# Last phase of a GNN + FFN kernel: VectorE's instruction for x2's mean is taken out, and two pieces of its step stand later

## Chip, core, metric

The kernel runs on one core of a Trainium2 chip. The metric is the device time of one execution in microseconds (us); it is given as the median of a few runs, and one further execution was taken with the hardware profiler.

## What is computed

10,000 nodes of 512 features pass a layer norm, three rounds of a graph network (a sum over each node's edges, two 512x512 products, ReLU, a norm over the row), and a residual sum. Then comes a feed-forward layer with 8 experts, of which each node takes its best two, a second residual sum, and a last layer norm inside it. Cut to what the change touches:

```python
def layer_norm(x, g, b):
    m = x.mean(-1, keepdims=True)
    v = ((x - m) ** 2).mean(-1, keepdims=True)
    return (x - m) / jnp.sqrt(v + EPS) * g + b
...
x = x + gnn(layer_norm0(x), src, dst, ...)       # this sum is x2 in the kernel
xn = layer_norm0(x)                              # mean and variance of x2
x = x + ffn(xn, Wg, W1, b1, W2, b2, ...)
```

## The kernel before

The edges are sorted by target node and cut into 79 tiles of 127 edges; all work goes tile by tile, 128 rows by 512 columns. Phases 0, 1 and 2 are the layer norm and the first graph rounds with their products. This case is about the last phase, number 3, from about 1490 us to the end: it sums the last round's rows, forms x2, and does the whole feed-forward layer.

Each engine has its own program, an unrolled loop over steps. In step k an engine calls a fixed list of small functions, each for the tile k plus an offset: the list `[(-9, hs), ..., (3, x2), ...]` at the end of VectorE's block is its order of a step, written out by hand. Engines meet only through semaphores (`wait_ge`, `then_inc`), and each runs its own instructions strictly in order. Tiles go in groups of four: some functions do a whole group at once, in the step in which its last tile comes by, so four steps in a row differ, and the pattern repeats every four.

What a step does, with the lines as the profile has them and the names of the tiles (buffers are reused, so a row of the trace may call x2's tile `area`, and the small scalars `w_n`):

- **POOL (GpSimd)**: `gather` (L814, rows of the neighbours by an indirect DMA), `by_node` (L830, rows of x; waits for an earlier tile's x2, whose buffer it refills), `norm3` (L881, and L883, which writes `scl`), once a group `pow_of_group` (L873, waits for `group_vars`), `zr_of` (L890, L893, which writes `zr`), `put_out` (L902, the result's rows, an indirect DMA that adds).
- **VectorE (DVE)**: `hs` (L1636), once a group `confidences` (L1618 to L1626, which writes W128), `carry_lo` (L1461), `combine` (L1473, writes R), `x2` (L1522: x2 = RR * scl + X, both in SBUF, with the row's sum as a second result, read out by a short instruction of its own), `x2_mean` (L1530), `logits` (L1573), `flo` (L1643, reads two SBUF tiles), once a group `group_scales` (L1558 to L1562), `largest` (L1580), `one_hot` (L1452), `largest_index` (L1586), once a group `gaps` and `group_vars` (L1542, L1544), then `z_stats` (L1648), `hots`, `z_mean_var` (L1654), `result` (L1671), `z_gain` (L1661), `xlo` (L1568).
- **ScalarE (ACT)**: `relu` (L994), `sum_squares3` (L1030), `weights_in` (L1072), `x2_deviations` (L1038: the squares of x2 less its mean, and their sum), `xn` (L1047), `xhi` (L1056), `gelu` (L1080), `carry_hi` (L983), `fhi` (L1087).
- **TensorE (PE)**: `aggregate` (L1827, L1828), `down` (L553 into psS, L1893, L1894), `turn_w` (L1856, which waits for W128), `up` (L1869, L1871), `gate` (L553 into psA), `spread_w` (L1879).

A loop between POOL and VectorE runs through this: `x2` waits for `scl` of its tile from POOL's L883, and POOL's L830, some instructions later, waits for an older x2. `down` waits for `flo`; `largest` waits for `logits`.

Of the kernel before, what the change touches and what calls it, by code (L numbers as in the profile page):

```python
# [5 lines left out]
ALU = mybir.AluOpType  # L6
ACT = mybir.ActivationFunctionType
# [10 lines left out]
D = 512  # L18
# [5 lines left out]
T = -(-E // EPT)  # L24
# [28 lines left out]
LN_EPS = 1e-5  # L53
# [69 lines left out]
def run_plan(tiles, stages, jobs, windows=(), run=0):  # L123
    offs = [o for o, _ in stages]
    begin, end = -max(max(offs), 0), max([tiles - min(min(offs), 0)] + [j[0] + 1 for j in jobs])
    cuts = sorted({begin, end} | {j[0] for j in jobs} | {e for w in windows for e in w[:2]})
    for a, b in zip(cuts, cuts[1:]):
        for at, f, arg in jobs:
            if at == a:
                f() if arg is None else f(arg)  # L130
        run_steps(tiles, stages + [(0, f) for x, y, f in windows if x <= a and b <= y], a, b, run)
# [28 lines left out]
def after(eng, sem, n):  # L160
    if n > 0:
        eng.wait_ge(sem, n)
# [57 lines left out]
class FfnSems:  # L220


    def __init__(self, sem):
        self.out = [sem(f"f3_out{i}") for i in range(2)]
        self.x2 = sem("f3_x2")
        self.mean = sem("f3_mean")
        self.dev = sem("f3_dev")
        self.ssf = sem("f3_ssf")
        self.lnv = sem("f3_lnv")
        self.pw = sem("f3_pw")  # L230
        self.nb = sem("f3_nb")
        self.xn = sem("f3_xn")
        self.xhi = sem("f3_xhi")
        self.xlo = sem("f3_xlo")
        self.ht = [sem(f"f3_ht{i}") for i in range(HT_RING)]
        self.gate = sem("f3_gate")
        self.logit = sem("f3_logit")
        self.top = sem("f3_top")
        self.topi = sem("f3_topi")
        self.gap = sem("f3_gap")  # L240
        self.hot = sem("f3_hot")
        self.th = sem("f3_th")
        self.w48 = sem("f3_w48")
        self.pad = sem("f3_pad")
        self.wt = sem("f3_wt")
        self.wtt = sem("f3_wtt")
        self.up = sem("f3_up")
        self.gel = sem("f3_gel")
        self.spread = sem("f3_spread")
        self.hs = sem("f3_hs")  # L250
        self.fhi = sem("f3_fhi")
        self.flo = sem("f3_flo")
        self.down = sem("f3_down")
        self.bnz = sem("f3_bnz")
        self.aggz = sem("f3_aggz")
        self.zv = sem("f3_zv")
        self.zr = sem("f3_zr")
        self.o1 = sem("f3_o1")
        self.prior = [sem(f"f3_prior{i}") for i in range(2)]
        self.o = sem("f3_o")  # L260


def build(nc, x, src, dst, W_self, W_neigh, b, Wg, W1, b1, W2, b2, ln_g, ln_b, out_g, out_b, out):
    with ExitStack() as ctx:
# [247 lines left out]
        def lt(n, dt=F32, parts=P):  # L512

            at = late_at[0]
            late_at[0] = at + n
            v = late[0:parts, at:at + n]
            return v if dt is F32 else v.bitcast(dt)

        sumx = lt(2 * GROUP).rearrange("p (i t) -> p i t", i=2)
        nmean = lt(2 * GROUP).rearrange("p (i t) -> p i t", i=2)  # L520
        ssx = lt(2 * GROUP).rearrange("p (i t) -> p i t", i=2)
        vvb = lt(4 * GROUP).rearrange("p (i t two) -> p i t two", i=2, two=2)
        pwb = lt(4 * GROUP).rearrange("p (i t two) -> p i t two", i=2, two=2)
# [389 lines left out]
        def _(act):  # L913
# [118 lines left out]
            def x2_deviations(t):  # L1032

                t = t.own
                i, j = t.group % 2, t.place
                act.wait_ge(f3.mean, (t + 1).n)
                after(act, f3.lnv, t.group - 1)
                act.activation(bmat.rearrange("p c n -> p (c n)"), X2[t.slot(X2_RING)], ACT.Square, bias=nmean[:, i, j:j + 1],  # L1038
                               accum_out=ssx[:, i, j:j + 1]).then_inc(f3.dev, 1)

            def xn(t):

# [51 lines left out]
        def _(dve):  # L1094
# [352 lines left out]
            def one_hot(t, l):  # L1447

                s = ph[l]
                i = t.slot(GRING)  # L1450
                after(dve, s.agg, (t + (1 - GRING)).n)
                dve.tensor_scalar(Sm[i][:, :], iota16[:, :], colT[:, t.t:t.t + 1], rowval[:, 0:1],  # L1452
                                  ALU.is_equal, ALU.mult).then_inc(s.smat, 1)

            def carry_lo(t, l):
                s = ph[l]
                i, o = t.slot(2), (t + 1).slot(GRING)
                if t.t == T - 1:
                    return
                dve.wait_ge(s.chi, (t + 1).n - t.run)  # L1460
                dve.scalar_tensor_tensor(G[o][0:1, D:2 * D], (psA3 if l == 3 else psA)[i][0:1, :], 1.0 / CARRY,  # L1461
                                         G[o][0:1, 0:D], ALU.mult, ALU.subtract).then_inc(s.clo, 1)

            def combine(t, l):
                s = ph[l]
                i = t.slot(2)
                if l == 1:
                    dve.wait_ge(s.x[i], t.landed(2))
                else:
                    dve.wait_ge(s.xs[i], Tile(t.t, l - 2).landed(2))  # L1470
                dve.wait_ge(s.agg, (t + 1).n)
                after(dve, s.rr, (t + -1).n)
                dve.scalar_tensor_tensor(R[i][:, :], (psA3 if l == 3 else psA)[i][:, :], invs[:, l - 1, t.t:t.t + 1],  # L1473
                                         Sl[i][:, :], ALU.mult, ALU.add).then_inc(s.r, 1)
# [40 lines left out]
            def x2(t):  # L1515
                i, q = t.slot(2), t.slot(X2_RING)
                dve.wait_ge(s.sc, (t + 1).n)
                dve.wait_ge(s.rr, (t + 1).n)
                t = t.own
                dve.wait_ge(s.xg[i], t.landed(2))  # L1520
                after(dve, f3.o, (t + (1 - X2_RING)).n)
                dve.scalar_tensor_tensor(X2[q], RR[i][:, :], scl[:, i:i + 1], X[i][:, :], ALU.mult, ALU.add,  # L1522
                                         accum_out=sumx[:, t.group % 2, t.place:t.place + 1]).then_inc(f3.x2, 1)

            def x2_mean(t):
                t = t.own
                i, j = t.group % 2, t.place
                dve.wait_ge(f3.x2, (t + 1).n)
                after(dve, f3.dev, GROUP * (t.group - 1))
                dve.tensor_scalar(nmean[:, i, j:j + 1], sumx[:, i, j:j + 1], -1.0 / D, None, ALU.mult  # L1530
                                  ).then_inc(f3.mean, 1)

            def group_vars(t):

                t = t.own
                if not t.ends_group:
                    return
                g, k = t.group, t.place + 1
                i = g % 2
                dve.wait_ge(f3.dev, (t + 1).n)  # L1540
                after(dve, f3.pw, g - 1)
                dve.tensor_scalar(vvb[:, i, 0:k, 0], ssx[:, i, 0:k], (1.0 + LN_EPS) / (D * LN_UP ** 2),  # L1542
                                  (LN_EPS / LN_UP) ** 2, ALU.mult, ALU.add)
                dve.tensor_scalar(vvb[:, i, 0:k, 1], ssx[:, i, 0:k], 1.0 / D, LN_EPS, ALU.mult, ALU.add  # L1544
                                  ).then_inc(f3.lnv, 1)

            def group_scales(t):

                t = t.own
                if not t.ends_group:  # L1550
                    return
                g, k = t.group, t.place + 1
                i, q = g % 2, g % 4
                dve.wait_ge(f3.pw, g + 1)

                after(dve, f3.xn, GROUP * (g - 1))
                after(dve, f3.zv, GROUP * (g - 3))
                link(dve.scalar_tensor_tensor(r2b[:, q, 0:k], pwb[:, i, 0:k, 1], 0.5 * CONF_UP / LN_UP, pwb[:, i, 0:k, 0],  # L1558
                                              ALU.mult, ALU.mult))
                dve.scalar_tensor_tensor(ezb[:, q, 0:k], r2b[:, q, 0:k], downs[:, FINAL:FINAL + 1], r2b[:, q, 0:k],  # L1560
                                         ALU.mult, ALU.mult)
                dve.tensor_tensor(nbb[:, i, 0:k], nmean[:, i, 0:k], pwb[:, i, 0:k, 0], ALU.mult).then_inc(f3.nb, 1)  # L1562

            def xlo(t):
                t = t.own
# [108 lines left out]
            def sev_last(k):  # L1674
                sev(late_tile(k, 2), 2)

            run_plan(T, [(-9, hs), (-5, confidences), (4, lambda t: carry_lo(t, 3)), (4, lambda t: combine(t, 3)), (3,
                          x2), (3, x2_mean), (-4, logits), (-9, flo), (2, group_scales), (-4, largest), (6, lambda t:
                          one_hot(t, 3)), (-4, largest_index), (-4, gaps), (3, group_vars), (-10, z_stats), (-4, hots),
                          (-10, z_mean_var), (-11, result), (-10, z_gain), (-1, xlo)],  # L1680
                     [(max(k - LATE_AHEAD, -1) - 3, sev_last, k) for k in range(LATE[2])], run=2)


# [247 lines left out]
```

## Time and profile before

| | us |
|---|---|
| median of 3 runs (lowest, highest) | 2128.86 (2127.16, 2131.32) |
| profiled execution, its own time | 2129.58 |
| span of that execution in the trace | 2127.5 |
| busy in the span: PE, DVE, ACT, POOL | 1992.0, 1671.8, 1015.8, 1269.9 |

The profiled execution's time is 2.08 us above its span, and 0.72 us above the median. Busy shares are means over phases with different limits; what matters below is read from the last phase alone.

### The profile page before, as it was taken

To read this page: it belongs to the slowest core of one execution; us is meant where nothing else is said; L and a number is where in the kernel's file an instruction comes from. 1 tells how busy PE (TensorE), PEld (TensorE's weight loads), DVE (VectorE), ACT (ScalarE), POOL (GpSimd) and SP (SyncE) were. 2 spreads that over 40 slices of the span, in tenths; PEclk is the share of its full clock that TensorE was granted. 3 is DMA by queue.
4 is the path that set the end of the run, shared out by engine and by line. 5 is a ranking of instruction groups with operands and counts; after the bars stand their busy time and mean duration, and the time that the engine had idled before them with its cause. 6 is when DMAs were issued, how large, how long until landed. Compare 5 with 4: busy or idle time off the path is not lost.

```text
span 2127.5 us, 42838 instructions
## 1 busy us (share of the span) xinstructions
PE 1992.0 (94%) x14663; PEld 1101.4 (52%) x14669; DVE 1671.8 (79%) x4112; ACT 1015.8 (48%) x1794; POOL 1269.9 (60%) x1396
## 2 busy tenths in 40 slices
PE   6999899997999999997999999988699999999996
PEld 3454444443444444443444444443477777777774
DVE  7778986655777787775888877775699999999985
ACT  4444333332444443343444434444777777677751
POOL 2884116784666666563444444443678888888865
PEclk9999999998999999999999999999899999999998
DMA  6664338974788777874788888874779998999963
GB/s 206 169 169 130 121 139 138 142 127 120 200 197 202 193 205 192 195 196 144 236 246 252 250 241 233 240 222 157 206 161 176 176 179 177 177 175 184 172 103 49
DMA packets 321183, 382.67 MB, mean 180 GB/s; under 512 B 190554, under 2 KB 190728, under 8 KB 320968
## 3 DMA queue, kind: packets, MB, share of 16 engines
q1 hardware_dynamic: 260151, 214.50, 43.3%
q0 software_dynamic: 60816, 165.43, 31.5%
q8 instruction: 119, 1.95, 0.4%
q14 instruction: 97, 0.79, 0.1%
HBM read 175.81 MB, written 165.31 MB: 160 GB/s over the span
## 4 chain that ended last, share of the span: by engine, by line
PE 45%; POOL 22%; issue 11%; DMA 9%; DVE 8%; ACT 4%; SPq 1%; POOLq 0%; DVEq 0%; ACTq 0%
PE psS L553 19%; PE psY L553 19%; DMA w_n<-HH 7%; POOL out_dram L902 4%; POOL node_info L737 4%; POOL X L830 3%; PE psT L1770 2%; POOL zr L893 2%; PE psY L1869 2%; POOL G L814 2%; POOL area L814 2%; DVE R L1473 2%; POOL scl L883 1%; POOL w_n L873 1%; PE psA L1828 1%
## 5 line engine op out<-in xcount | busy, mean ns | idle before, releaser
L553 PE MATMUL psY<-w_n,HT 128*128 128x512 f16 x1812 | 423.0, 384 | 11.8 <-ACT HT L967 9.1
L553 PE MATMUL psS<-w_s,HT 128*128 128x512 f16 x1812 | 415.8, 379 | 1.4 <-DVE SB L1364 1.4
L553 PEld LDWEIGHTS psY<-w_n,HT 128*128 128x128 f16 x1812 | 177.7, 99 | 231.9 <-ACT HT L967 12.8
L994 ACT ACTIVATE RR<-R 128x512 f32<-128x512 f32 x237 | 149.5, 631 | 304.9 <-DVE R L1473 304.8
L846 POOL DMA_INDIRECT y_rows<-YB,poutT x158 | 161.4, 1021 | 193.2 <-DVE YB L1352 161.0
L553 PEld LDWEIGHTS psS<-w_s,HT 128*128 128x128 f16 x1812 | 173.8, 98 | 197.3 <-DVE SB L1364 1.9
L1364 DVE SCALAR_TENSOR_TENSOR SB<-psS,downs,bias 128x512 f32<-128x512 f32 x237 | 177.7, 750 | 79.2 <-PE psS L553 77.2
L839 POOL TENSOR_TENSOR scl<-ssm,halfpow 128x1 f32<-128x1 f32 x158 | 88.6, 561 | 223.0 <-DVE ssm L1491 223.0
L553 PE MATMUL psS<-w_w,raw 128*128 128x512 f16 x948 | 217.6, 379 | 0.8 <-ACT raw L1087 0.8
L553 PE MATMUL psY<-w_n 128*128 128x512 f16 x852 | 195.8, 380 | 13.6 <-DMA w_n<-HH 13.3
L1352 DVE SCALAR_TENSOR_TENSOR YB<-psY,YB 128x512 f16<-128x512 f32 x237 | 162.5, 685 | 54.3 <-ACT YB L960 53.5
L553 PE MATMUL psS<-w_s,w_n 128*128 128x512 f16 x852 | 195.5, 379 | 0.0
L1005 ACT ACTIVATE HH<-RR,scl 128x512 f16<-128x512 f32 x158 | 114.1, 722 | 150.1 <-POOL scl L839 150.1
L960 ACT ACTIVATE YB<-psY 128x512 f16<-128x512 f32 x237 | 138.2, 583 | 70.9 <-PE psY L553 60.6
L1497 DVE SCALAR_TENSOR_TENSOR HH<-RR,scl,HH 128x512 f16<-128x512 f32 x158 | 118.7, 751 | 57.4 <-ACT HH L1005 57.4
L951 ACT ACTIVATE HH<-R 128x512 f16<-128x512 f32 x79 | 49.7, 629 | 225.3 <-DVE R L1328 225.3
L902 POOL DMA_INDIRECT out_dram<-raw,poutT x79 | 147.3, 1864 | 15.3 <-issue 14.5
L814 POOL DMA_INDIRECT G<-y_rows,srcT x120 | 126.9, 1058 | 48.9 <-issue 31.2
L553 PEld LDWEIGHTS psS<-w_w,raw 128*128 128x128 f16 x948 | 92.0, 98 | 109.8 <-ACT raw L1087 1.1
L758 POOL TENSOR_TENSOR scl<-ssm,halfpow 128x1 f32<-128x1 f32 x79 | 61.6, 781 | 145.3 <-DVE ssm L1321 140.1
L1473 DVE SCALAR_TENSOR_TENSOR R<-psA,invs,Sl 128x512 f32<-128x512 f32 x198 | 144.4, 729 | 0.7 <-DMA Sl<-self_rows,pinT 0.7
L553 PEld LDWEIGHTS psY<-w_n 128*128 128x128 f16 x852 | 81.0, 98 | 120.7 <-DMA w_n<-HH 27.0
(327 smaller groups left out, 4094.6 us busy)
## 6 DMA issues: line engine op xcount, KB each, us to landing
self_rows<-SB SPq DMA_DIRECT2D x236, 256.0 KB, 2.0
Sl<-self_rows SPq DMA_DIRECT2D x158, 256.0 KB
area<-in_x_dram SPq DMA_DIRECT2D x78, 256.0 KB, 4.7
y_rows<-YB SPq DMA_DIRECT2D x78, 256.0 KB, 4.5
out_dram<-obb SPq DMA_DIRECT2D x78, 256.0 KB, 4.3
raw<-in_L_gnn_W_neigh_dram SPq DMA_DIRECT2D x12, 256.0 KB, 3.8
raw<-in_L_gnn_W_self_dram SPq DMA_DIRECT2D x12, 256.0 KB
y_rows<-YB,poutT POOLq DMA_INDIRECT x158
```

The costliest lines, as they stand in the source:

```text
L553: mm = eng.matmul(acc, lhs[:, a, c, :], w[:, bpart, c, :], start=(c == 0 and n == 0), stop=(stop and c == KC - 1 and n == 2))
L814: pool.indirect_dma_start(G[i][:, :], None, Yd[l - 1][:, :], bass.IndirectOffsetOnAxis(ap=srcT[:, t.t:t.t + 1], axis=0), bounds_check=node ...
L839: pool.tensor_tensor(scl[:, i:i + 1], ssm[:, i:i + 1], halfpow[:, 1:2], ALU.pow).then_inc(s.sc, 1)
L846: pool.indirect_dma_start(Yd[l][:, :], bass.IndirectOffsetOnAxis(ap=poutT[:, t.t:t.t + 1], axis=0), YB[i][:, :], None, bounds_check=node_l ...
L902: pool.indirect_dma_start(out[:, :], bass.IndirectOffsetOnAxis(ap=poutT[:, t.t:t.t + 1], axis=0), OUT[i], None, bounds_check=node_limit, o ...
L960: act.activation(YB[i][:, 0:D], psY[i][:, :], ACT.Copy, scale=k).then_inc(s.yhi, 1)
L994: act.activation(RR[i][:, :], R[i][:, :], ACT.Relu).then_inc(s.rr, 1)
L1005: act.activation(HH[i][:, 0, :], RR[i][:, :], ACT.Copy, scale=scl[:, i:i + 1]).then_inc(s.hhi, 1)
L1352: dve.scalar_tensor_tensor(YB[i][:, D:2 * D], psY[i][:, :], k, YB[i][:, 0:D], ALU.mult, ALU.subtract).then_inc(s.ylo, 1)
L1364: dve.scalar_tensor_tensor(SB[i][:, :], psS[i][:, :], downs[:, c:c + 1], bias[:, l, :], ALU.mult, ALU.add).then_inc(s.sev, 1)
L1473: dve.scalar_tensor_tensor(R[i][:, :], (psA3 if l == 3 else psA)[i][:, :], invs[:, l - 1, t.t:t.t + 1], Sl[i][:, :], ALU.mult, ALU.add).th ...
L1497: dve.scalar_tensor_tensor(HH[i][:, 1, :], RR[i][:, :], scl[:, i:i + 1], HH[i][:, 0, :], ALU.mult, ALU.subtract).then_inc(s.hlo, 1)
```

## The change

The mean of x2 is no longer formed. ScalarE squares the sum less 512 times the value, which is the deviation times 512 with its sign turned; `group_vars` divides by 512 cubed in place of 512, and `group_scales` multiplies the sum by -1/512 where it took the mean. ScalarE now waits for x2's semaphore. In VectorE's list, `x2` moves from behind `combine` to behind `flo`, and `group_vars` from ahead of `z_stats` to behind `z_gain`.

```diff
-                act.wait_ge(f3.mean, (t + 1).n)
+                act.wait_ge(f3.x2, (t + 1).n)
                 after(act, f3.lnv, t.group - 1)
-                act.activation(bmat.rearrange("p c n -> p (c n)"), X2[t.slot(X2_RING)], ACT.Square, bias=nmean[:, i, j:j + 1],
-                               accum_out=ssx[:, i, j:j + 1]).then_inc(f3.dev, 1)
+                act.activation(bmat.rearrange("p c n -> p (c n)"), X2[t.slot(X2_RING)], ACT.Square, bias=sumx[:, i, j:j + 1],
+                               scale=-float(D), accum_out=ssx[:, i, j:j + 1]).then_inc(f3.dev, 1)
...
                 after(dve, f3.o, (t + (1 - X2_RING)).n)
+                after(dve, f3.dev, GROUP * (t.group - 1))
                 dve.scalar_tensor_tensor(X2[q], RR[i][:, :], scl[:, i:i + 1], X[i][:, :], ALU.mult, ALU.add,
                                          accum_out=sumx[:, t.group % 2, t.place:t.place + 1]).then_inc(f3.x2, 1)
-
-            def x2_mean(t):
-                t = t.own
-                i, j = t.group % 2, t.place
-                dve.wait_ge(f3.x2, (t + 1).n)
-                after(dve, f3.dev, GROUP * (t.group - 1))
-                dve.tensor_scalar(nmean[:, i, j:j + 1], sumx[:, i, j:j + 1], -1.0 / D, None, ALU.mult
-                                  ).then_inc(f3.mean, 1)
...
-                dve.tensor_scalar(vvb[:, i, 0:k, 0], ssx[:, i, 0:k], (1.0 + LN_EPS) / (D * LN_UP ** 2),
+                dve.tensor_scalar(vvb[:, i, 0:k, 0], ssx[:, i, 0:k], (1.0 + LN_EPS) / (D ** 3 * LN_UP ** 2),
...
-                dve.tensor_tensor(nbb[:, i, 0:k], nmean[:, i, 0:k], pwb[:, i, 0:k, 0], ALU.mult).then_inc(f3.nb, 1)
+                dve.scalar_tensor_tensor(nbb[:, i, 0:k], sumx[:, i, 0:k], -1.0 / D, pwb[:, i, 0:k, 0],
+                                         ALU.mult, ALU.mult).then_inc(f3.nb, 1)
...
-            run_plan(T, [(-9, hs), (-5, confidences), (4, lambda t: carry_lo(t, 3)), (4, lambda t: combine(t, 3)), (3,
-                          x2), (3, x2_mean), (-4, logits), (-9, flo), (2, group_scales), (-4, largest), (6, lambda t:
-                          one_hot(t, 3)), (-4, largest_index), (-4, gaps), (3, group_vars), (-10, z_stats), (-4, hots),
-                          (-10, z_mean_var), (-11, result), (-10, z_gain), (-1, xlo)],
+            run_plan(T, [(-9, hs), (-5, confidences), (4, lambda t: carry_lo(t, 3)), (4, lambda t: combine(t, 3)), (-4, logits), (-9, flo), (3, x2), (2, group_scales), (-4, largest), (6, lambda t:
+                          one_hot(t, 3)), (-4, largest_index), (-4, gaps), (-10, z_stats), (-4, hots),
+                          (-10, z_mean_var), (-11, result), (-10, z_gain), (3, group_vars), (-1, xlo)],
```

The first place is on VectorE, in the step in which a group's variances are formed, in the middle of the last phase. Before (L1522 is `x2`, L1530 the mean, L1573 `logits`, L1643 `flo`, L1542 and L1544 `group_vars`, L1671 `result`):

```order
L1522 SCALAR_TENSOR_TENSOR area,w_n<-RR,scl,X 128x512
L1530 TENSOR_SCALAR w_n<-w_n 128x1
L1573 SCALAR_TENSOR_TENSOR w_n<-psA,downs,bgb 128x8
L1643 TENSOR_TENSOR raw<-raw 128x512
L1580 MAX w_n<-w_n 128x8
L1452 TENSOR_SCALAR Sm<-iota,colT,rowval 128x128
L1586 MAX_INDEX w_n<-w_n 128x8
L1542 TENSOR_SCALAR w_n<-w_n 128x4
L1544 TENSOR_SCALAR w_n<-w_n 128x4
L1648 BN_STATS st6b<-psS 128x6
L1654 BN_AGGR zm<-st6b 128x2
L1671 SCALAR_TENSOR_TENSOR raw<-area,zr 128x512
```

The same place now. Line numbers have shifted: `logits` is L1565, `flo` L1635, `x2` L1521, `result` L1663, `z_gain` L1653, `group_vars` L1533 and L1535:

```order
L1565 SCALAR_TENSOR_TENSOR w_n<-psA,downs,bgb 128x8
L1635 TENSOR_TENSOR raw<-raw 128x512
L1521 SCALAR_TENSOR_TENSOR area,w_n<-RR,scl,X 128x512
L1572 MAX w_n<-w_n 128x8
L1450 TENSOR_SCALAR Sm<-iota,colT,rowval 128x128
L1578 MAX_INDEX w_n<-w_n 128x8
L1640 BN_STATS st6b<-psS 128x6
L1646 BN_AGGR zm<-st6b 128x2
L1663 SCALAR_TENSOR_TENSOR raw<-area,zr 128x512
L1653 SCALAR_TENSOR_TENSOR area<-psS,zm,ogb 128x512
L1533 TENSOR_SCALAR w_n<-w_n 128x4
L1535 TENSOR_SCALAR w_n<-w_n 128x4
```

`logits` and `flo` now come ahead of `x2`, one instruction is gone, and the variances have moved behind four more instructions.

The second place is on VectorE one step later, where the group's scales are formed (L1558 to L1562). Before, from `combine` on:

```order
L1473 SCALAR_TENSOR_TENSOR R<-psA,invs,Sl 128x512
L1522 SCALAR_TENSOR_TENSOR area,w_n<-RR,scl,X 128x512
L1530 TENSOR_SCALAR w_n<-w_n 128x1
L1573 SCALAR_TENSOR_TENSOR w_n<-psA,downs,bgb 128x8
L1643 TENSOR_TENSOR raw<-raw 128x512
L1558 SCALAR_TENSOR_TENSOR w_n<-w_n 128x4
```

And now (`combine` is L1471, the scales begin at L1549):

```order
L1471 SCALAR_TENSOR_TENSOR R<-psA,invs,Sl 128x512
L1565 SCALAR_TENSOR_TENSOR w_n<-psA,downs,bgb 128x8
L1635 TENSOR_TENSOR raw<-raw 128x512
L1521 SCALAR_TENSOR_TENSOR area,w_n<-RR,scl,X 128x512
L1549 SCALAR_TENSOR_TENSOR w_n<-w_n 128x4
```

The scales stood behind `flo` and now stand right behind `x2`; `x2` has `flo` right ahead of it. The programs of ScalarE, POOL, TensorE and SyncE keep their order.

## Rows read from the trace of the kernel before

**Rows 1.** Busy us (instructions) of each engine, granted clock, DMA, 1600 to 2000 us.

```profile
core 0: us, PE busy (x) PEld busy (x) DVE busy (x) ACT busy (x) POOL busy (x), PEclk, DMA share, GB/s
1600.00:2000.00 400.00, 387.53 (x4959) 289.89 (x4957) 382.00 (x1102) 282.46 (x605) 346.64 (x389) 1.00 0.95 178
```

**Rows 2.** TensorE's waits from 1600 us on: total us, times, longest.

```profile
PE psT L1856 <- DVE w_n L1626: 13.4, 14, 1.2
```

**Rows 3.** VectorE's waits, 1600 to 2010 us.

```profile
DVE area L1522 <- POOL scl L883: 6.9, 14, 0.5
DVE w_n L1542 <- ACT bmat L1038: 4.1, 14, 0.3
```

**Rows 4.** POOL's waits, 1600 to 2010 us (one of four lines, all of this kind).

```profile
POOL out_dram L902 <- issue: 10.2, 55, 0.2
...
```

**Rows 5.** Timeline of POOL, `pow_of_group`, first and last full group: start, us.

```profile
1607.25 1.64 POOL L873 TENSOR_TENSOR w_n<-w_n,powers 128x8 f32<-128x8 f32 x1
...
1995.03 1.64 POOL L873 TENSOR_TENSOR w_n<-w_n,powers 128x8 f32<-128x8 f32 x1
```

**Rows 6.** Timeline of TensorE, the starts of two successive `down`.

```profile
1857.00 2.75 PE L553 MATMUL psS<-w_w,raw 128*128 128x512 f16 x12
...
1864.17 2.75 PE L553 MATMUL psS<-w_w,raw 128*128 128x512 f16 x12
```

**Rows 7.** Timeline of POOL within one group.

```profile
1854.11 0.58 POOL L883 TENSOR_TENSOR scl<-ssm,halfpow 128x1 f32<-128x1 f32 x1
...
1855.09 0.84 POOL L893 TENSOR_TENSOR zr<-zv,halfpow 128x1 f32<-128x1 f32 x1
1856.11 1.87 POOL L902 DMA_INDIRECT out_dram<-raw,poutT  x1 [0.18 <-issue]
...
1861.05 0.57 POOL L883 TENSOR_TENSOR scl<-ssm,halfpow 128x1 f32<-128x1 f32 x1
...
1869.04 0.57 POOL L893 TENSOR_TENSOR zr<-zv,halfpow 128x1 f32<-128x1 f32 x1
1869.79 2.17 POOL L902 DMA_INDIRECT out_dram<-raw,poutT  x1 [0.18 <-issue]
```

**Rows 8.** Timeline of VectorE in the same group.

```profile
1854.72 0.77 DVE L1522 SCALAR_TENSOR_TENSOR area<-RR,scl,X 128x512 f32<-128x512 f32 x1 [0.49 <-POOL scl L883]
1855.43 0.08 DVE L1522 DVE_READ_ACCUMULATOR area<-RR,scl,X 128x1 f32 x1
1855.54 0.15 DVE L1530 TENSOR_SCALAR w_n<-w_n 128x1 f32<-128x1 f32 x1
1855.61 0.21 DVE L1573 SCALAR_TENSOR_TENSOR w_n<-psA,downs,bgb 128x8 f32<-128x8 f32 x1
1855.74 0.68 DVE L1643 TENSOR_TENSOR raw<-raw 128x512 f16<-128x512 f32 x1
1856.34 0.16 DVE L1580 MAX8 w_n<-w_n 128x8 f32<-128x8 f32 x1
...
1860.79 0.73 DVE L1473 SCALAR_TENSOR_TENSOR R<-psT,invs,Sl 128x512 f32<-128x512 f32 x1
1861.65 0.78 DVE L1522 SCALAR_TENSOR_TENSOR area<-RR,scl,X 128x512 f32<-128x512 f32 x1
...
1869.01 0.73 DVE L1473 SCALAR_TENSOR_TENSOR R<-psA,invs,Sl 128x512 f32<-128x512 f32 x1
1869.66 0.73 DVE L1522 SCALAR_TENSOR_TENSOR area<-RR,scl,X 128x512 f32<-128x512 f32 x1
...
1876.88 0.73 DVE L1522 SCALAR_TENSOR_TENSOR area<-RR,scl,X 128x512 f32<-128x512 f32 x1
```

**Rows 9.** Timelines of VectorE and POOL elsewhere: L883 under a VectorE instruction, L902 alone.

```profile
1567.15 0.73 DVE L1671 SCALAR_TENSOR_TENSOR raw<-area,zr 128x512 f32<-128x512 f32 x1
...
1567.30 1.02 POOL L883 TENSOR_TENSOR scl<-ssm,halfpow 128x1 f32<-128x1 f32 x1
...
2095.10 1.62 POOL L902 DMA_INDIRECT out_dram<-raw,poutT  x1 [0.19 <-issue]
```

More of the change, by code:

```diff
@@ L225, in __init__ @@
         self.x2 = sem("f3_x2")
-        self.mean = sem("f3_mean")
         self.dev = sem("f3_dev")
@@ L519, in build @@
         sumx = lt(2 * GROUP).rearrange("p (i t) -> p i t", i=2)
-        nmean = lt(2 * GROUP).rearrange("p (i t) -> p i t", i=2)
         ssx = lt(2 * GROUP).rearrange("p (i t) -> p i t", i=2)
@@ L1541, in group_vars @@
                 after(dve, f3.pw, g - 1)
-                dve.tensor_scalar(vvb[:, i, 0:k, 0], ssx[:, i, 0:k], (1.0 + LN_EPS) / (D * LN_UP ** 2),
+                dve.tensor_scalar(vvb[:, i, 0:k, 0], ssx[:, i, 0:k], (1.0 + LN_EPS) / (D ** 3 * LN_UP ** 2),
                                   (LN_EPS / LN_UP) ** 2, ALU.mult, ALU.add)
-                dve.tensor_scalar(vvb[:, i, 0:k, 1], ssx[:, i, 0:k], 1.0 / D, LN_EPS, ALU.mult, ALU.add
+                dve.tensor_scalar(vvb[:, i, 0:k, 1], ssx[:, i, 0:k], 1.0 / D ** 3, LN_EPS, ALU.mult, ALU.add
                                   ).then_inc(f3.lnv, 1)
```

## The prediction

> **What bounds the kernel now.** I read the busy shares of the last phase first. From 1600 to 2000 us TensorE is busy for 387.5 of 400 us and VectorE for 382 [rows 1], both at the full 2.4 GHz grant. That names two candidates and decides nothing, so I went to the waits of each engine. TensorE stalls 14 times, 13.4 us in all, each time at `turn_w` for W128 from VectorE [rows 2]: once a group. VectorE waits 6.9 us in 14 places for `scl` from POOL, and 4.1 us in 14 for ScalarE's sum of squares in `group_vars` [rows 3]. POOL waits for nobody: all four lines of its waits read "issue", gaps that follow each of its DMA instructions [rows 4]. So although POOL has the lowest busy figure of the three, it sets the pace: POOL delays `x2`, VectorE then delays W128, TensorE stalls. The pace is 13 groups between the first and the last `pow_of_group`, (1995.03 - 1607.25) / 13 = 29.83 us a group [rows 5]. TensorE alone would need 4 x 7.17 = 28.68 [rows 6]. The difference, 1.15 us a group, is all that any change outside TensorE can return here: 14 x 1.15, some 16 us.
>
> **Why POOL's instructions differ in length.** The same `zr` instruction takes 0.57 us at 1869.04 and 0.84 at 1855.09 [rows 7]. In the second case `x2`, which reads two SBUF tiles, is running until 1855.49 [rows 8], and `zr` ends 0.44 later. `put_out` takes 1.62 alone [rows 9], 1.87 at 1856.11 with `flo` running until 1856.42, and 2.17 at 1869.79 with `x2` until 1870.39 [rows 7, 8]: both end 1.56 to 1.57 after the VectorE instruction. `scl` took 1.02 instead of 0.57 when `result`, running to 1567.88, covered its start: it ended 0.44 after it [rows 9]. So a POOL instruction that starts under a VectorE instruction with two SBUF inputs is held until that one ends. This coupling decides the case, because the change moves `x2` against `flo`, and POOL's pace follows. By the Trainium skill (SBUF — State Buffer, Who interferes with whom), a VectorE instruction with two SBUF inputs contends with GpSimd instructions that read SBUF, and the page infers that descriptor generation, which needs the write side, is not stalled by a tensor_tensor. The first half agrees with `zr`'s 0.84 against 0.57; the second does not agree with `put_out`'s 1.87 against 1.62 under a tensor_tensor. By the page taken alone, moving `flo` away from `put_out` would return nothing there; by the rows it returns 0.25 in each of two steps of a group.
>
> **The change part by part.** (a) The mean: from the read-out of `x2`'s sum to `logits` is 0.18 us, of which the mean's own start-to-start is 0.07 [rows 8]. The read-out stays, so the saving lies between 0.07 and 0.18; I take 0.12, four times a group. (b) `logits` and `flo` ahead of `x2`: 0.13 and 0.60 by their starts [rows 8]. In the step at 1854.72 VectorE stands 0.49 us for `scl`; it can now do these two in that time. (c) `group_vars` behind `z_gain`: its wait of 4.1 / 14 = 0.29 goes. Its result then comes at most 3.7 us after `x2` (`x2` to `largest` 0.77, `largest` to `combine` 1856.34 to 1860.79, less three instructions of over 0.5 that stay behind it). (d) ScalarE's square has the same size, and `group_scales` the same count; I cost them at nothing. `flo` and `logits` come earlier, so TensorE, which waits for them, gains cover. Later is `x2`, for `by_node` on POOL and the squares on ScalarE. POOL runs more than a step behind here (it waits for no semaphore [rows 4]). Before POOL is saturated it does wait for `x2`, once, so its whole chain may start up to 0.73 later; against that, from `scl` to W128 VectorE now has `logits`, `flo` and the mean less, 0.85. I net these to nothing.
>
> **VectorE's new pace.** `x2` to `x2` over the four steps is 6.93, 8.01, 7.22 and, by the repeat after 29.81, 7.65 [rows 8]. Out of these come waits: 0.21 in the first (`combine` to `x2` is 0.86 there, 0.65 at 1869.01), 0.35 in the third (c, with the gap beside it), 0.55 in the fourth (0.49 and the same gap), and the mean's 0.12 in each: 6.60, 7.89, 6.75, 6.98, sum 28.22. This is below TensorE's 28.68.
>
> **POOL against it.** Put 0 at the end of the `scl` instruction at 1854.69, and count on.
> - Second step. `x2` starts at 0.03 and holds `zr`, which ends at 1.24 as before; `put_out` starts at 1.42, no longer under `flo`, and takes 1.62. From its end to the next `scl` instruction is 1861.05 - 1857.98 = 3.07 [rows 7], so that starts at 6.11. `flo` now stands 0.60 ahead of `x2`: it starts at 0.03 + 6.60 - 0.60 = 6.03, and runs to 6.71. The `scl` instruction starts under it, and ends at 6.71 + 0.44 = 7.15. `x2` starts at 7.18 where it could have at 6.63: a new wait of 0.55, made by the move itself.
> - Third step. `x2` comes at 7.18 + 7.89 = 15.07, `flo` at 14.47; the `scl` instruction starts at 7.15 + 6.11 = 13.26 and is clear. `put_out` starts 1.14 after its end (0.39 + 0.57 + 0.18), under `flo`, and ends at 16.7, or at 17.4 if it has to let `x2` pass too.
> - Fourth step. The `scl` instruction starts 3.07 later, at 19.8 or 20.5; `flo` comes at 21.2: clear. `pow_of_group` (1.64 [rows 5]) follows at 20.4 or 21.0; the variances are there by 15.07 + 3.7 = 18.8. `x2` at 21.82.
> - First step of the next group. `x2` holds POOL until 22.56, `put_out` starts near 23.55, the `scl` instruction 1.62 + 3.07 later at 28.24. `flo` starts at 21.82 + 6.98 - 0.60 = 28.20. These are 0.04 apart, less than I know them. If it is held, `x2` comes at 29.35; if not, at 28.80.
>
> So a group costs 28.22 plus 0.55 for each step in which `flo` covers the start of the `scl` instruction, and no less than 28.68. No such step: 28.68, a gain of 1.15 a group. One: 28.77, gain 1.06. Two: 29.32, gain 0.51. Three: 29.87, no gain. Four: 30.42, a loss of 0.59. The working gives one for certain and a second on a knife's edge, so I take it in half of the groups: 0.78 a group, times 13, is 10.2 us. From the profiled execution (2129.58) that makes 2119.4; against the median, which is 0.72 lower, 2118.7. I say 2119.
>
> **Rivals.** *TensorE takes over.* If POOL's and VectorE's phases settle so that `flo` misses the `scl` instruction, both lie below 28.68, and the stall at `turn_w` is gone: 13 to 14 groups x 1.15, 2113 to 2114. For it: only 0.08 separates the two starts in the second step. Against: the delay is self-repairing, since after a hit both move on by the same amount, and meet again. *Nothing comes of it.* POOL's chain is full, what the change removes is on VectorE, and `put_out`'s saving is paid back by `flo` in front of `scl`: three hits a group, 2129 to 2130. For it: every wait removed is on an engine that does not set the pace. *Slower.* `flo` and `x2` side by side hold POOL for 1.3 us in a row where two shorter stretches stood apart; if `flo` meets `scl` in all four steps, 13 x 0.59 = 8 us more, 2137. It decides from the fourth hit on; against it stands the third step, where `confidences` pushes `flo` 1.2 us past. A price without a row here is that of POOL slipping in between `flo` and `x2`: nothing, or the 0.66 of `put_out` above, which the next hit swallows.
>
> **How the numbers follow.** About 0.2% (4.3 us) is what a measurement of this kernel can tell from no change. TensorE's pace 0.28; one or two hits a group, the forecast, 0.40; nothing 0.19; slower 0.13. Faster is the first two, 0.68; same 0.19; slower 0.13. The forecast's own range is 2114.5 to 2122.5 (one hit to two in each group). The range to be held reaches from TensorE's floor to just past no gain, 2113 to 2131.
>
> **What would show it.** Right: the pitch of `pow_of_group` falls from 29.83 to 28.8 to 29.3; TensorE's stalls at `turn_w` shrink from 0.96 to between 0.1 and 0.6; `put_out` behind the first step's `x2` is 1.6; some `scl` instructions read about 1.1 instead of 0.57, each with `flo` over its start; the wait of L1542 for ScalarE is gone. If no `scl` is long and TensorE stands for nobody, the first rival holds. If POOL still shows no wait and 29.8, the second. The prediction is wrong at its root if POOL's instructions keep their lengths whatever VectorE runs beside them.

## The result, and the profile after

The changed kernel is slower: 2156.99 us (median; 2155.21 to 2161.5) against 2128.44 (the three runs ahead of the prediction and a fourth), a ratio of 1.0133 (95% interval 1.0116 to 1.015). The forecast was 2119, with a range of 2113 to 2131. In the profiled execution the span grew from 2127.5 to 2153.2 us. `pow_of_group` (now L871) is again once a group:

```profile
1639.66 1.64 POOL L871 TENSOR_TENSOR w_n<-w_n,powers 128x8 f32<-128x8 f32 x1
...
1987.47 1.64 POOL L871 TENSOR_TENSOR w_n<-w_n,powers 128x8 f32<-128x8 f32 x1
```

Eleven groups lie between these two, so a group takes 31.62 us where it took 29.83 [rows 5]. Over the 13 or so groups of the steady stretch that is 23 of the span's 25.7 us. The busy shares of 1600 to 2000 us, and the waits of TensorE, VectorE and POOL in 1600 to 2010 (total, times, longest):

```profile
1600.00:2000.00 400.00, 370.16 (x4673) 275.22 (x4671) 354.62 (x987) 273.27 (x571) 349.50 (x367) 1.00 0.93 167
```

```profile
PE psT L1847 <- DVE w_n L1618: 21.8, 12, 1.8
```

```profile
DVE area L1521 <- POOL scl L881: 30.5, 39, 0.8
DVE w_n L1549 <- POOL w_n L871: 11.3, 13, 0.9
```

```profile
POOL out_dram L900 <- issue: 9.6, 52, 0.2
```

Against [rows 1 to 4]: TensorE and VectorE lost 17 and 27 us of work in the same 400 us, POOL gained 3. `x2` now waits for `scl` in three steps of every four, 0.78 us each time (30.5 / 39), where it waited once a group, 0.49. `group_scales` (L1549) waits for the power, 0.87 a group, which it never did. The variances' wait for ScalarE is gone, as forecast. POOL still waits for nothing that the profile shows.

Its instructions changed in length. POOL's groups from 1600 to 2000 us (busy us, mean ns), of the changed kernel and then of before:

```profile
L812 POOL DMA_INDIRECT G<-y_rows,srcT x26 | 40.3, 1550 | 7.9 <-issue 7.9
L888 POOL TENSOR_SCALAR zv<-zm,w_n 128x1 f32<-128x1 f32 x51 | 38.1, 748 | 0.5
L879 POOL TENSOR_SCALAR ssm<-ss 128x1 f32<-128x1 f32 x50 | 21.2, 424 | 1.4
```

```profile
L814 POOL DMA_INDIRECT G<-y_rows,srcT x26 | 28.1, 1082 | 7.9 <-issue 7.9
L890 POOL TENSOR_SCALAR zv<-zm,w_n 128x1 f32<-128x1 f32 x54 | 17.2, 318 | 0.5
L881 POOL TENSOR_SCALAR ssm<-ss 128x1 f32<-128x1 f32 x53 | 16.7, 314 | 1.5
```

Where they are held is seen in the timelines, POOL first, then VectorE (`x2` L1521, `xlo` L1560, `combine` L1471, `logits` L1565, `flo` L1635):

```profile
1806.15 0.58 POOL L881 TENSOR_TENSOR scl<-ssm,halfpow 128x1 f32<-128x1 f32 x1
...
1808.14 1.69 POOL L900 DMA_INDIRECT out_dram<-raw,poutT  x1 [0.18 <-issue]
1810.14 1.55 POOL L812 DMA_INDIRECT G<-y_rows,srcT  x1 [0.31 <-issue]
...
1813.03 0.43 POOL L879 TENSOR_SCALAR ssm<-ss 128x1 f32<-128x1 f32 x1
1813.54 0.57 POOL L881 TENSOR_TENSOR scl<-ssm,halfpow 128x1 f32<-128x1 f32 x1
...
1820.89 2.05 POOL L888 TENSOR_SCALAR zv<-zm,w_n 128x1 f32<-128x1 f32 x1
...
1828.91 0.57 POOL L881 TENSOR_TENSOR scl<-ssm,halfpow 128x1 f32<-128x1 f32 x1
1829.47 1.64 POOL L871 TENSOR_TENSOR w_n<-w_n,powers 128x8 f32<-128x8 f32 x1
```

```profile
1806.76 0.77 DVE L1521 SCALAR_TENSOR_TENSOR area<-RR,scl,X 128x512 f32<-128x512 f32 x1 [0.79 <-POOL scl L881]
...
1810.05 0.68 DVE L1560 TENSOR_TENSOR HH<-area,HH 128x512 f16<-128x512 f32 x1
...
1812.70 0.67 DVE L1635 TENSOR_TENSOR raw<-raw 128x512 f16<-128x512 f32 x1
1814.15 0.78 DVE L1521 SCALAR_TENSOR_TENSOR area<-RR,scl,X 128x512 f32<-128x512 f32 x1 [0.78 <-POOL scl L881]
...
1820.63 0.73 DVE L1471 SCALAR_TENSOR_TENSOR R<-psA,invs,Sl 128x512 f32<-128x512 f32 x1
1821.29 0.20 DVE L1565 SCALAR_TENSOR_TENSOR w_n<-psA,downs,bgb 128x8 f32<-128x8 f32 x1
1821.42 0.67 DVE L1635 TENSOR_TENSOR raw<-raw 128x512 f16<-128x512 f32 x1
1822.02 0.73 DVE L1521 SCALAR_TENSOR_TENSOR area<-RR,scl,X 128x512 f32<-128x512 f32 x1
...
1829.52 0.75 DVE L1521 SCALAR_TENSOR_TENSOR area<-RR,scl,X 128x512 f32<-128x512 f32 x1 [0.78 <-POOL scl L881]
...
1831.15 0.16 DVE L1549 SCALAR_TENSOR_TENSOR w_n<-w_n 128x4 f32<-128x4 f32 x1 [0.87 <-POOL w_n L871]
...
1838.26 0.77 DVE L1521 SCALAR_TENSOR_TENSOR area<-RR,scl,X 128x512 f32<-128x512 f32 x1 [0.79 <-POOL scl L881]
```

Three places. (1) `flo` runs to 1813.37; `ssm`, begun under it, ends 0.09 later, then come 0.08, `scl` 0.57 and 0.04 until `x2`: the 0.78. (2) `gather` starts under `xlo`, 1.55 for 1.08, in two of a group's four gathers (those into G). (3) In the step with `confidences` VectorE is late and `scl` in time, but `zv` begins under `combine`, with `flo` and `x2` behind it without a gap, and ends 0.19 after `x2` does: 2.05 for 0.30.

### The profile page after: what moved, and what is told of

It is laid out like the page before. It is cut to its first block, busy times and chain, and to the rows that moved or that the text cites. A ratio compares the mean times of both kernels' runs of the same rounds, so it can differ in the third digit from the quotient of the medians.

```text
span 2153.2 us, 42696 instructions
## 1 busy us (share of the span) xinstructions
PE 1995.7 (93%) x14663; PEld 1103.4 (51%) x14669; DVE 1662.2 (77%) x4033; ACT 1022.9 (48%) x1794; POOL 1296.8 (60%) x1396
## 4 chain that ended last, share of the span: by engine, by line
PE 47%; POOL 24%; issue 9%; DMA 8%; DVE 6%; ACT 4%; SPq 1%; POOLq 0%; DVEq 0%; ACTq 0%
PE psS L551 20%; PE psY L551 20%; DMA w_n<-HH 6%; POOL out_dram L900 5%; POOL node_info L735 4%; POOL X L828 3%; POOL G L812 2%; PE psT L1761 2%; POOL zv L888 2%; PE psY L1860 2%; POOL area L812 2%; POOL zr L891 2%; DVE R L1471 1%; POOL scl L881 1%; POOL ssm L879 1%
## 5 line engine op out<-in xcount | busy, mean ns | idle before, releaser
L812 POOL DMA_INDIRECT G<-y_rows,srcT x120 | 141.3, 1178 | 54.0 <-issue 30.8
L812 POOL DMA_INDIRECT area<-y_rows,srcT x117 | 127.2, 1087 | 30.6 <-issue 30.6
L1471 DVE SCALAR_TENSOR_TENSOR R<-psA,invs,Sl 128x512 f32<-128x512 f32 x198 | 144.4, 729 | 0.6 <-DMA Sl<-self_rows,pinT 0.6
```

Source lines behind the costliest of these rows:

```text
L812: pool.indirect_dma_start(G[i][:, :], None, Yd[l - 1][:, :], bass.IndirectOffsetOnAxis(ap=srcT[:, t.t:t.t + 1], axis=0), bounds_check=node ...
```

## The experiments

A hold is the time by which a POOL instruction lasts longer than it does alone. The "holds theory" of the expectations is that VectorE instructions with two SBUF inputs cause these holds, and that they, through POOL's pace, made the changed kernel slower.

The table gives each kernel's ratio to before and, from its trace, the mean group (distance of the `pow_of_group` rows between 1620 and 2015 us), x2's wait for `scl` (us, times, 1600 to 2010), and POOL's holds a group: every POOL instruction's length less its length alone (`ssm` 0.27, `scl` 0.57, the power 1.64, `zv` 0.30, `zr` 0.57, `put_out` 1.62, `gather` 1.07, `by_node` 1.00). The group less the holds is 27.2 in every kernel with `ssm` and 25.6 to 25.8 without: POOL's gaps never change. That sum holds whatever the cause is; what tells causes apart is which holds and waits go with which edit.

| kernel | ratio (95%) | group | x2's wait | holds |
|---|---|---|---|---|
| before | 1 | 29.83 | 6.9, 14 | 2.60 |
| changed | 1.0133 (1.0116 to 1.015) | 31.62 | 30.5, 39 | 4.40 |
| x2_back | 1.0005 (0.9986 to 1.0025) | 29.85 | 17.7, 13 | 2.62 |
| x2_only | 1.0159 (1.013 to 1.0187) | 32.22 | 24.7, 36 | 4.97 |
| vars_only | 0.9977 (0.9962 to 0.9991) | 29.45 | 6.9, 14 | 2.22 |
| xlo_first | 1.0211 (1.0189 to 1.0233) | 32.63 | 28.0, 36 | 5.39 |
| flo_one | 0.9993 (0.9975 to 1.0012) | 29.67 | 16.4, 27 | 2.43 |
| scales_later | 1.013 (1.0112 to 1.0148) | 31.72 | 27.6, 37 | 4.49 |
| no_floor | 1.0059 (1.0042 to 1.0076) | 30.62 | 18.4, 39 | 4.82 |
| xlo_one | 1.01 (1.0076 to 1.0124) | 31.43 | 30.3, 39 | 4.19 |
| mean_only | 1.0024 (1.0005 to 1.0043) | 30.14 | 19.0, 14 | 2.90 |
| x2_back_pad | 0.9987 (0.9968 to 1.0005) | 29.48 | 6.9, 14 | 2.24 |
| vars_no_floor | 0.9942 (0.9923 to 0.9961) | 28.81 | none | 3.22 |
| x2_back_no_floor | 0.9948 (0.9932 to 0.9965) | 28.62 | 7.1, 14 | 3.05 |

**Which part costs.** x2_back takes the changed kernel and puts `x2` back; x2_only takes before and moves `x2` (with its mean) alone; vars_only moves the variances alone.

```diff
-(-4, logits), (-9, flo), (3, x2), (2, group_scales)      # x2_back, from the changed kernel
+(3, x2), (-4, logits), (-9, flo), (2, group_scales)
-(3, x2), (3, x2_mean), (-4, logits), (-9, flo)           # x2_only, from before
+(-4, logits), (-9, flo), (3, x2), (3, x2_mean)
-(3, group_vars), (-10, z_stats), ... (-10, z_gain), (-1, xlo)    # vars_only, from before
+(-10, z_stats), ... (-10, z_gain), (3, group_vars), (-1, xlo)
```

> The changed kernel with x2 back ahead of logits and flo; no mean, and the variances stay late. Holds theory (the new place of x2 lays POOL's gather under xlo, 1.55 us for 1.08, and POOL's zv under flo and x2 side by side, 2.05 for 0.30; POOL's chain sets the pace): x2 to xlo goes back to about 4.1 us, gather starts under z_gain again and takes 1.08, zv 0.30, and the group falls from 31.5 to between 28.7 and 29.8 us, the time to 2113 to 2129. Rival, the mean or the late variances are the cause: the group stays above 31 and the time above 2145.

> The kernel before with one edit, x2 and its mean moved behind flo; the variances stay early. Holds theory: gather falls under xlo and zv under flo and x2, the group takes 31 to 31.7 us, the time 2145 to 2158. Rival, the removed mean or the late variances are the cause: 2124 to 2133.

> The kernel before with one edit, the group's variances behind z_gain. Holds theory: POOL sets the pace and its holds stay, so 2124 to 2130, and the 0.29 us wait of the variances for ScalarE, once a group, is gone. Rival, late variances make POOL's power late and VectorE's scales wait for it (0.87 us a group in the changed kernel): 2135 to 2142.

Measured: 2133.12, 2163.71 and 2124.9 us. The move of `x2` is the whole loss and more; the late variances help a little, as expected, and the rival of a late power falls. x2_only lies 6 us above its range, and its holds are not those that were expected: `zv` is free (0.04 a group), `gather` has 0.59, and in their place `zr` has 1.91 (in one step of four it now starts where `zv` did, under `combine` with `flo` and `x2` behind), `ssm` 1.05 and `scl` 1.04. So it is the move of `x2` that costs, but which POOL instruction is held depends on the rest of the order. x2_back missed its 2129 by 4 us and has its `gather` held after all (below); its groups, 29.85, are those of before.

**Does a hold's second input matter?** flo_one and xlo_one leave VectorE's order as changed, and give one instruction a single SBUF input: bn_stats, which reads one tile for its mean and variance and writes 128x6.

```diff
-dve.tensor_tensor(FH[i][:, 1, :], HS[i], FH[i][:, 0, :], ALU.subtract).then_inc(f3.flo, 1)   # flo_one
+dve.bn_stats(st6c[:, :], HS[i]).then_inc(f3.flo, 1)
-dve.tensor_tensor(HH[i][:, 1, :], XN[i], HH[i][:, 0, :], ALU.subtract).then_inc(f3.xlo, 1)   # xlo_one
+dve.bn_stats(st6c[:, :], XN[i]).then_inc(f3.xlo, 1)
```

> The changed kernel in its own order, but flo replaced from the third tile on by a bn_stats over HS, which reads one SBUF tile and should last as long; the low half of the second product's input is left out (the old bytes stay). Over the four kernels so far the group of POOL is 27.5 us plus the sum of its holds. Holds theory: without a second SBUF input flo holds nothing, zv 0.30 for 2.05, ssm 0.27 for 0.42, and the group falls from 31.5 to 28.7 to 29.7 us, the time to 2113 to 2130. Rival, the order as such (x2 one instruction later, its wait for scl): 31 us or more, 2148 or more.

Measured: 2128.41, the loss gone. Timelines of POOL and of VectorE in flo_one (`combine` L1472, bn_stats in flo's place L1639, `x2` L1522), the same place as (3):

```profile
1808.53 0.30 POOL L889 TENSOR_SCALAR zv<-zm,w_n 128x1 f32<-128x1 f32 x1
1808.91 0.57 POOL L892 TENSOR_TENSOR zr<-zv,halfpow 128x1 f32<-128x1 f32 x1
```

```profile
1808.29 0.73 DVE L1472 SCALAR_TENSOR_TENSOR R<-psA,invs,Sl 128x512 f32<-128x512 f32 x1
...
1809.08 0.67 DVE L1639 BATCH_NORM_STATS2 st6c<-raw 128x6 f32<-128x512 f32 x1
1809.68 0.72 DVE L1522 SCALAR_TENSOR_TENSOR area<-RR,scl,X 128x512 f32<-128x512 f32 x1
```

`zv` begins 0.24 after `combine` (0.26 in the changed kernel), VectorE's instructions stand at the same distances and last as long, and it takes 0.30, not 2.05. So `flo` holds POOL; neither `combine` nor the order does. The bn_stats drops flo's 128x512 output as well as its second SBUF input, but `combine`, which reads PSUM and one SBUF tile, writes as large a tile to SBUF, and the `zv` that starts under it here is free; `x2`, the same operation with both tiles in SBUF, holds (`zr` 0.84 for 0.57, [rows 7, 8]). That leaves the second input. The Trainium skill (SBUF — State Buffer, Who interferes with whom) says that a VectorE instruction with two SBUF inputs contends with a GpSimd instruction that reads SBUF, and one with a single input, outside the two-port modes, does not: this pair agrees.

> The changed kernel in its own order, but xlo replaced from the third tile on by a bn_stats over XN, which reads one SBUF tile and lasts about as long; the low half of the first product's input is left out (the old bytes stay). First form of the holds theory, the holds simply add up: gather 1.08 for 1.55 takes 1.17 us a group away, 30.4 and 2140 to 2146. Revised form, after the run with xlo first: whatever POOL's instruction ahead of x2 finds free before it, it is held until flo ends, so x2's wait is pinned at what then remains of ssm and scl, 0.78, in three steps of four; gather 1.08, but ssm 0.9 to 1.25 in place of 0.42, the group stays at 31.3 to 32, 2150 to 2162.

Measured: 2152.81, a group of 31.43. Timelines of POOL and VectorE in xlo_one (`flo` L1639 again):

```profile
1813.30 1.08 POOL L813 DMA_INDIRECT G<-y_rows,srcT  x1 [0.31 <-issue]
...
1815.72 0.90 POOL L880 TENSOR_SCALAR ssm<-ss 128x1 f32<-128x1 f32 x1
```

```profile
1815.86 0.67 DVE L1639 TENSOR_TENSOR raw<-raw 128x512 f16<-128x512 f32 x1
1817.30 0.78 DVE L1522 SCALAR_TENSOR_TENSOR area<-RR,scl,X 128x512 f32<-128x512 f32 x1 [0.77 <-POOL scl L882]
```

`gather` is free, 1.08, and POOL reaches `ssm` half a microsecond sooner, only to be held until `flo` ends: 0.90 for 0.43, and `x2` waits 0.77 as ever. The first form of my theory, that holds add up, falls here; the revised form stands: `x2` is pinned to flo's end. Across the changed kernel, xlo_one and xlo_first, `x2` has to wait for `scl` in 114 places between 1600 and 2010 us; `ssm` starts there anywhere from 0.53 before flo's start to 0.34 behind it, and the wait is 0.77 to 0.79 each time. The pin has an edge: in x2_only, in one step of four, an `ssm` that starts 0.93 to 0.95 before `flo` is free, the `scl` behind it is held instead (1.69 to 1.70 for 0.57), and `x2` waits 0.47.

**The order of xlo and of the scales.** xlo_first is the run that had forced that revision.

```diff
-(-11, result), (-10, z_gain), (3, group_vars), (-1, xlo)     # xlo_first, from the changed kernel
+(-11, result), (-1, xlo), (-10, z_gain), (3, group_vars)
-(2, group_scales), (-4, largest), ... (-4, largest_index), (-4, gaps)    # scales_later
+(-4, largest), ... (-4, largest_index), (2, group_scales), (-4, gaps)
```

> The changed kernel with xlo ahead of z_gain, so that the instruction over the start of POOL's gather reads one SBUF tile and PSUM. Holds theory: gather 1.08 for 1.55, ssm then starts 0.5 earlier, clear of flo, but scl starts under flo and is held instead (about 1.0 for 0.57): 0.3 us a step less in three steps of four, the group 30.6, the time some 12 us less, 2141 to 2149. Rival, the wait of x2 is the fixed price of flo standing ahead of it (ssm held whatever POOL did before): 31.5 a group and 2154 to 2159.

Measured: 2174.76, a group of 32.63: the theory's range and the rival's are both missed. VectorE's waits there:

```profile
DVE area L1521 <- POOL scl L881: 28.0, 36, 0.8
DVE w_n L1549 <- POOL w_n L871: 12.0, 13, 1.5
DVE HH L1560 <- ACT HH L1054: 11.1, 37, 0.4
```

The rival's half was right: 0.78 for `x2` (28.0 / 36) whatever `gather` did, as in this step (POOL, then `flo` L1635 and `x2` on VectorE), where `ssm` came 0.49 ahead of `flo` and was held to 0.09 past its end:

```profile
1709.67 1.25 POOL L879 TENSOR_SCALAR ssm<-ss 128x1 f32<-128x1 f32 x1
```

```profile
1710.16 0.67 DVE L1635 TENSOR_TENSOR raw<-raw 128x512 f16<-128x512 f32 x1
1711.61 0.75 DVE L1521 SCALAR_TENSOR_TENSOR area<-RR,scl,X 128x512 f32<-128x512 f32 x1 [0.78 <-POOL scl L881]
```

`gather` itself was not freed as expected: three of a group's four still start under `xlo` and take 1.30 to 1.33. On top, `xlo` came too early for ScalarE's high half, 0.30 a step, which I had not priced.

> The changed kernel with group_scales behind largest_index instead of right behind x2, so that VectorE does not stand 0.87 us a group for POOL's power. Holds theory: VectorE's wait only moves, to x2 for scl; the group stays at 31 to 32 us, 2149 to 2162. Rival, VectorE's own waits make the time: 0.87 a group comes back, 30.65 and 2145 or less.

Measured: 2159.18, a group of 31.72, in the ranges of the holds theory: the wait for the power halved (5.6 us in 13) and nothing came back. But the wait did not move to `x2`, whose own fell to 27.6 us. `carry_lo` now waits 8.2 us for ScalarE, and ScalarE 23.1 us for gathered rows to land, where these were 1.4 and 5.5 in the changed kernel. So the run does not isolate what the power's wait costs.

**Shorter work on POOL.** no_floor (from the changed kernel) and vars_no_floor (from vars_only) take `ssm` out:

```diff
-pool.tensor_scalar(ssm[:, i:i + 1], ss[:, i:i + 1], 1e-24, None, ALU.max).then_inc(f3.ssf, 1)
-pool.wait_ge(f3.ssf, o.t + 1)
-pool.tensor_tensor(scl[:, i:i + 1], ssm[:, i:i + 1], halfpow[:, 1:2], ALU.pow).then_inc(s.sc, 1)
+pool.tensor_tensor(scl[:, i:i + 1], ss[:, i:i + 1], halfpow[:, 1:2], ALU.pow).then_inc(s.sc, 1)
...
-act.activation(junk[:, :], RR[i][:, :], ACT.Square, accum_out=ss[:, i:i + 1])
+act.activation(junk[:, :], RR[i][:, :], ACT.Square, bias=tiny[:, 0:1], accum_out=ss[:, i:i + 1])
```

> The changed kernel with POOL's ssm (the floor under the sum of squares) taken out: ScalarE's squares get a bias of 1e-13 instead, so that no sum is zero, and POOL has one instruction a tile less, 0.35 us with its gap. Holds theory: 1.4 us a group less of POOL's work, the holds about as they are: 30 to 30.4 us, 2135 to 2142. Rival, VectorE's order sets the pace whatever POOL has to do: 31.5 and 2157.

> The kernel before with the late variances (2125 us, 29.43 a group, holds of 1.9) and without POOL's ssm, as in the run beside it. Holds theory: 27.5 - 1.4 + 1.9 = 28.0 us for POOL, under TensorE's 28.68: TensorE sets the pace, its stall at W128 goes, 2110 to 2117. Rival, the holds grow as POOL moves and eat it: 29 us or more, 2119 or more.

Measured: 2143.18 and 2119.15. In no_floor, VectorE waits:

```profile
DVE area L1521 <- POOL scl L881: 18.4, 39, 0.5
DVE w_n L1549 <- POOL w_n L873: 12.9, 14, 1.5
```

POOL lost 1.4 us of work a group and the group only 1.00, just short of what the holds theory expected (30 to 30.4 us, 2135 to 2142). The pin explains it: now `scl` itself is held, 0.44 remain behind flo's end and 0.04 to `x2`, 0.48 by that sum and 0.47 measured; VectorE's own 28.28 (below) + 3 x 0.47 + 0.92 (12.9 / 14) = 30.61, and 30.62 was measured. vars_no_floor missed its bound by 2 us and met the rival's 2119, and the rival's mechanism is there in part: the holds grew from 2.22 to 3.22 a group. Its group, 28.81, is TensorE's pace all the same, and not the rival's 29: TensorE is busy for 399.5 of the 400 us, and its only stall left at `turn_w` is 0.2 us.

**The mean.** mean_only takes the mean out of before and moves nothing. x2_back_pad puts the mean's instruction back into x2_back, its result unread.

```diff
-(3, x2), (-4, logits), (-9, flo)              # x2_back_pad, from x2_back
+(3, x2), (3, unused_mean), (-4, logits), (-9, flo)
```

> The kernel before with the mean taken out and nothing moved. Holds theory: VectorE's 0.12 a step is not on the way, but xlo comes nearer to x2 and gather under it or under result: 29.7 to 30.2 a group, 2127 to 2134. Rival, the saving counts in full, 4 x 0.12 a group: 29.35, 2121 to 2124.

> The run with x2 back (no mean, late variances, 29.85 a group, 2133) with one 128x1 instruction put where the mean stood, whose result nobody reads. Holds theory: the run with the late variances alone had 29.45 a group; the difference is that without the mean POOL's gather falls under result and xlo (holds of 0.99 a group against 0.06), so an idle instruction of 0.1 us makes it faster: gather 1.08 again, 29.4 to 29.5 a group, 2123 to 2128. Rival, ScalarE's scaled square or the sum's reader costs the 0.4: 29.85 stays.

Measured: 2135.01 and 2127.68. Taking out 0.12 us a step did not make the kernel faster but, by its interval, 0.05 to 0.43% slower (1 us past the expected range); by groups it costs 0.31 (30.14 against 29.83), and the idle instruction returns 0.37 (29.48 against 29.85). In mean_only `zv` is held 0.68 a group more than before and `gather` 0.50, `zr` 0.51, `put_out` 0.21 and `ssm` 0.14 less. The intervals of x2_back and x2_back_pad overlap, so their times alone do not tell them apart; the groups do, with one trace of each. Timeline of x2_back, `xlo` (L1560) and `gather`, and then of x2_back_pad (`xlo` L1567):

```profile
1802.46 0.68 DVE L1560 TENSOR_TENSOR HH<-area,HH 128x512 f16<-128x512 f32 x1
...
1802.56 1.55 POOL L812 DMA_INDIRECT G<-y_rows,srcT  x1 [0.30 <-issue]
```

```profile
1799.60 1.07 POOL L813 DMA_INDIRECT G<-y_rows,srcT  x1 [0.31 <-issue]
...
1800.24 0.68 DVE L1567 TENSOR_TENSOR HH<-area,HH 128x512 f16<-128x512 f32 x1
```

Without the idle instruction `gather` starts 0.10 behind xlo's start and is held; with it, 0.64 ahead, and is free.

**A version that beats both.** x2_back_no_floor keeps the removed mean and the late variances, has `x2` back ahead of `flo`, and no `ssm`: its edits are those of x2_back and no_floor.

> The run with x2 back, and POOL's ssm taken out as in the two runs before. Holds theory: POOL 27.23 - 1.6 + 2.6 = 28.2 at most, under TensorE's 28.68: 28.7 to 28.9 a group, 2113 to 2120. Rival, the holds grow as POOL moves and eat the gain: 29.2 a group or more, 2123 or more.

Measured: 2118.45, in the range and 0.5% under before; vars_no_floor cannot be told from it. The busy shares of 1600 to 2000 us in x2_back_no_floor:

```profile
1600.00:2000.00 400.00, 400.00 (x5134) 301.37 (x5133) 388.77 (x1090) 298.75 (x628) 349.68 (x350) 1.00 1.00 184
```

TensorE is busy all 400 us: the bound that the prediction put at 28.68 a group is reached, at 28.62.

## Why the prediction was wrong

**VectorE's own pace was right.** The prediction gave 6.60, 7.89, 6.75, 6.98, sum 28.22. From `x2` to `x2` the changed kernel takes 7.39, 7.87, 7.50, 8.74; less the waits (0.78; none; 0.78; 0.79 and 0.87) 6.61, 7.87, 6.72, 7.08, sum 28.28. The mean's 0.12 is in these numbers, and worth nothing in the time: mean_only. (The full grant in the prediction's first lines is TensorE's clock, and says nothing of VectorE's.)

**The term that failed is "0.55 for each step in which `flo` covers the start of the `scl` instruction", taken one and a half times a group.** The mechanism was the one that happens, but its size and count were wrong. What `flo` covers is `ssm`, one instruction earlier, so 0.78 is left, and it happens in three steps of four. 28.28 + 0.78 + 0.78 + 0.79 + 0.87 = 31.50: the five `x2` starts above span 31.50. Against the forecast's 28.22 + 1.5 x 0.55 = 29.05 that is 2.45 more: 1.5 from this term, 0.87 from the wait for the power, and the rest VectorE's own. (By its own gains times 13 the prediction's range for one to two hits is 2115.1 to 2122.2, where it wrote 2114.5 to 2122.5; nothing hangs on it.)

**Why so often.** I treated a meeting as chance, by two free-running phases, and wrote of "a knife's edge" and of 0.04. But POOL arriving early is stopped until flo's end, too (xlo_one, 0.90), so an arrival anywhere from half a microsecond ahead of `flo` (0.53 at most) to 0.34 behind its start gives the same 0.78. I had the reason in hand, as an argument against the first rival, that "the delay is self-repairing" and they meet again; it is a lock, and I gave it the price of an accident.

**"From its end to the next scl instruction is 3.07", carried over from before, failed as well**: 1813.54 - 1809.83 = 3.71, since the move brought `xlo` nearer to `x2` and over `gather` (0.47 of the 0.64), and `ssm` is held by 0.16. The hold of `gather` alone was not the cause (xlo_one).

**The third and fourth steps failed on `zv`.** I had `put_out` held under `flo` there; instead `zv` was held through `flo` and `x2`, 1.75 more, so that `scl` came at 22.18 on the prediction's clock (1828.91 - 1806.73) where it said 19.8 or 20.5, and the step was hit as well.

**The power** was put at nothing: (d) priced `group_scales` by its count of instructions, and the working gave the power's start and length but did not set its end against `group_scales`. With `x2` pinned to `scl`, the power begins at that same moment, and `group_scales`, right behind `x2`, meets its last 0.87. It goes with the hold: in flo_one, with `group_scales` in the same place, 0.22 is left (3.1 us in 14). What it costs by itself stays open, since scales_later removed half of it but brought other waits.

**The rivals.** "Slower" named the right place and the right direction, with four hits at 0.55 for 2137 and a chance of 0.13. "TensorE takes over" is what x2_back_no_floor does. That POOL's lack of waits makes it the pace-setter was read too simply: a held instruction is a wait that the list of waits doesn't name. The changed kernel's 31.50 is POOL's work and holds, and as well VectorE's work and its waits for POOL: the two pace each other.

## What to carry to other kernels

Before an instruction that waits for GpSimd, don't put a VectorE instruction with two SBUF inputs: here it held back the very work that was waited for, and the handover started only at its end, in three steps of four. An engine without waits in the profile may still be waiting: compare one instruction's length from step to step. Where two engines run this close, 0.1 us taken out of one is no gain by itself (mean_only); look at which pairs it lays over each other.

## What was not expected of the hardware

By the starts in the profile, the hold reaches ahead of the instruction that causes it, and over two that follow each other. `zv` began 0.53 us before `flo` and ended 0.19 after `x2`; with bn_stats in flo's place, 0.30. How far ahead it reaches, and on what that depends, is not settled: in x2_only a `scl` that began 0.58 to 0.59 before `flo`, and alone would have been over by then, took 1.69 to 1.70; but where `x2` stands right behind `combine`, in vars_no_floor, a `zv` that began 0.19 before `x2` took 0.31, and in the changed kernel one that begins 0.02 before `x2` takes 0.30.

DMA instructions on POOL are held too. `gather` took 1.55 under the two-input `xlo` and 1.08 in the same place under the one-input bn_stats. The Trainium skill (SBUF — State Buffer, Who interferes with whom) infers that descriptor generation, which needs the write side, is not stalled by a tensor_tensor; here the measurement differs, and decides. These DMAs also take their row numbers from SBUF (`srcT`, and `poutT` for the `put_out` of the prediction), so no run here tells whether it is the reading of these or the descriptors that is held.
